# The zeros written ahead of the last 46 row gathers of a mixture-of-experts kernel are left out

## The reference

```python
h = _L0_tok_ref(x, w, b, gamma, beta, alpha)      # depthwise conv (5 taps, stride 2), group norm, PReLU
h = h + _L0_attn_ref(_layernorm(h), ...)          # state space scan over the positions, 16 states a channel
h = h + _L0_ffn_ref(_layernorm(h), ...)           # 64 experts, the two best for each token

# _L0_ffn_ref, for a token row xf:
logits = xf @ Wr + br
topk_logits, topk_idx = top_k(logits, 2)
gates = softmax(topk_logits)
y_e = relu(xf @ W1[e] + b1[e]) @ W2[e] + b2[e]    # for each chosen expert e
out = sum over the two chosen e of gate_e * y_e
```

## Time and profile before

| | before |
|---|---|
| median of three runs | 925.29 us |
| lowest and highest run | 922.06, 929.41 us |
| the profiled execution | 921.33 us |
| its span, first to last instruction | 919.6 us |
| busy in the span: POOL, DVE, PE, ACT | 71%, 62%, 60%, 36% |
| the 46 gathers of the third share, first start to last start | 840.64 to 909.36 us |
| last instruction of DVE ends | 912.56 us |

### The profile page before, as it was taken

How to read it: one execution, slowest core, us unless ns; L and a number is a source line. 1 busy time by engine, 2 the same in 40 slices (tenths; PEclk the granted TensorE clock), 3 DMA queues, 4 the chain that set the end, 5 groups by cost and what they waited for, 6 DMA issues and landing times.

```text
span 919.6 us, 9334 instructions
## 1 busy us (share of the span) xinstructions
PE 555.3 (60%) x2514; PEld 372.0 (40%) x2520; DVE 568.8 (62%) x1180; ACT 332.5 (36%) x622; POOL 654.9 (71%) x645
## 2 busy tenths in 40 slices
PE   4653347575674575768556756577679765794230
PEld 4642012122221221244324545565568554683230
DVE  1697899999999999876464511132234211247964
ACT  2169756466466554342132111122224211241010
POOL 5894699999999999706848888763740387503884
PEclk9967576898798887775767667798799875797565
DMA  7999900000000000002600344467578844651012
GB/s 238 384 156 116 44 0 0 0 0 0 0 0 0 1 0 0 0 1 75 162 14 26 112 137 131 129 171 206 151 207 227 240 133 119 173 151 43 22 56 70
DMA packets 106607, 84.98 MB, mean 92 GB/s; under 512 B 30464, under 2 KB 90240, under 8 KB 106560
## 3 DMA queue, kind: packets, MB, share of 16 engines
q1 hardware_dynamic: 79312, 54.76, 27.4%
q10 hardware_dynamic: 19184, 21.40, 7.4%
q0 software_dynamic: 8064, 8.27, 3.4%
HBM read 57.22 MB, written 33.49 MB: 99 GB/s over the span
## 4 chain that ended last, share of the span: by engine, by line
PE 32%; POOL 30%; issue 16%; DVE 10%; another core or an unknown queue 4%; ACT 4%; SPq 1%; DMA 1%; POOLq 0%; ACTq 0%; DVEq 0%
PE ps L894 15%; POOL x_w L570 12%; POOL w_ring L563 11%; PE ps L881 6%; POOL xt L634 5%; PE ps L870 2%; PE ps L659 2%; PE ps L723 1%; PE ps L750 1%; POOL beat L633 1%; PE ps L808 1%; PE ps L745 1%; DVE lstat L1280 1%; DVE mi L1498 1%
## 5 line engine op out<-in xcount | busy, mean ns | idle before, releaser
L723 PE MATMUL ps<-x_w,ident 128*128 128x512 f32 x252 | 154.3, 771 | 102.0 <-POOL x_w L570 102.0
L563 POOL TENSOR_TENSOR w_ring<-xt,bc 128x2016 f32<-128x2016 f32 x32 | 144.7, 4524 | 13.4 <-DVE hh_ring L1409 7.3
L634 POOL DMA_INDIRECT xt<-expert_out,slot_i x126 | 123.6, 981 | 37.0 <-issue 21.9
L613 POOL DMA_INDIRECT sorted_rows<-xp,slot_i x126 | 123.0, 976 | 35.9 <-issue 18.4
L1409 DVE TENSOR_TENSOR_SCAN hh_ring<-ps,w_ring 128x1024 f32<-128x1024 f32 x64 | 145.7, 2277 | 0.1
L570 POOL TENSOR_TENSOR x_w<-hh_ring,bc 128x2016 f32<-128x2016 f32 (+1 forms) x32 | 142.4, 4456 | 2.3 <-PE ps L723 2.3
L723 PEld LDWEIGHTS ps<-x_w,ident 128*128 128x128 f32 x252 | 60.0, 249 | 199.0 <-POOL x_w L570 125.7
L633 POOL MEMSET beat<- 128x128 f32 x126 | 27.5, 218 | 106.3 <-DMA expert_out<-x_w 106.1
L1603 DVE COPY x_w<-ps 128x256 f32<-128x256 f32 x80 | 33.9, 424 | 109.2 <-PE ps L894 58.8
L1060 ACT ACTIVATE ps<-dt_t,a_exp 128x1024 f32<-128x1024 f32 x64 | 71.5, 1117 | 63.7 <-DVE hh_ring L1409 63.6
L1054 ACT ACTIVATE ps<-dt_t,a_exp 128x1024 f32<-128x1024 f32 x64 | 71.5, 1118 | 51.9 <-DVE w_ring L1388 51.9
(11 more groups left out here) (211 smaller groups left out, 956.1 us busy)
## 6 DMA issues: line engine op xcount, KB each, us to landing
dt_t<-packed SPq DMA_DIRECT2D x140, 96.5 KB
x_w<-packed SPq DMA_DIRECT2D x112, 96.5 KB
x_w<-sorted_rows ACTq DMA_DIRECT2D x40, 256.0 KB
expert_out<-x_w ACTq DMA_DIRECT2D x80, 128.0 KB
sorted_rows<-pad_rows SPq DMA_DIRECT2D x2, 3584.0 KB, 24.2
bc<-packed SPq DMA_DIRECT2D x68, 96.5 KB
packed<-in_L_ffn_W SPq DMA_DIRECT2D x3, 2048.0 KB, 39.4
x_w<-in_x SPq DMA_DIRECT2D x7, 448.0 KB, 9.8
```

Source lines behind the costliest of these rows:

```text
L563: pool.tensor_tensor(w_buf(k, 2), up3[:, bass.ds(c * DC, DC), 1:S].unsqueeze(1).broadcast_to([P, 2, DC, L]), vec_of(k, 2), ALU.mult).then_ ...
L613: pool.indirect_dma_start(out=sorted_rows[h], out_offset=bass.IndirectOffsetOnAxis(ap=slot_i[:, c, l:l + 1], axis=0), in_=xn[:, l, :], in_ ...
L634: pool.indirect_dma_start(out=y[:, l, :], out_offset=None, in_=expert_out[h], in_offset=bass.IndirectOffsetOnAxis(ap=slot_i[:, c, l:l + 1] ...
L723: ins = pe.matmul(ps[:, i, :], ident[:, :], src[:, i * BANK:(i + 1) * BANK], start=(k < 0), stop=(k == (N - 2 if last else N - 1)), skip_g ...
```

## The change

The memset of `beat`, with its semaphore and wait, is left out ahead of the 46 gathers of the third share. The 46 gathers themselves, their order and their semaphores stay. The memsets ahead of the 126 sends and of the 80 gathers of the first two shares stay.

```diff
                         for l in range(a, z):
-                            ch.link(pool.memset(beat[:, :], 0.0))
+                            if h + 1 < len(SHARES):
+                                ch.link(pool.memset(beat[:, :], 0.0))
                             pool.indirect_dma_start(
                                 out=y[:, l, :], out_offset=None, in_=expert_out[h],
                                 in_offset=bass.IndirectOffsetOnAxis(ap=slot_i[:, c, l:l + 1], axis=0)
```

## The result

| | before | after |
|---|---|---|
| median of four runs | 925.9 us | 950.24 us |
| lowest and highest run | 922.06, 929.41 us | 948.70, 951.99 us |
| the profiled execution, its span | 921.33, 919.6 us | 950.14, 948.4 us |

The ratio is 1.0264, with a 95% interval of 1.0219 to 1.0309. The change makes the kernel 24.3 us slower; I had forecast 5 us less.

What follows compares the result with a forecast made beforehand. It took the end as a race that POOL's gathers lose to DVE by 5.07 us, DVE's chain then being the bound: 921.33 − 5.07 = 916.26 us, against the median 925.29 − 5.07 = 920.2 us; range 916 to 952.

Steps and rivals of the forecast that it cites:

- POOL: Third share's gathers: 46 memsets (10.1 us) and the gaps behind them (13.3 us) go, 23.4 us of POOL's time.
- the short end I chose: POOL, gather period: of bounds 0.957 and 2.62 us, the side of 0.957, the shortest gather record.
- the second possibility: POOL, gather period: 0.957 + 0.27 = 1.23 us if the release gap stays; DVE is then the bound.
- The rival of slower bare gathers: POOL, between gathers: directly following gathers are slower, over 1% from a period of 1.73 us, 49 us at 2.62; chance 0.40.
- p: POOL, third share: period from one gather's start to the next, 1.527 us before; up to 1.41 the full 5.07 is saved.
- Today's period: POOL: a gather needs 1.45 us whatever stands ahead; 921.8 us, up to 934.5; chance 0.10 for periods 1.41 to 1.73.
- DVE's waits for gathers: DVE, last group of three positions: two waits, 1.30 + 3.77 = 5.07 us, are saved.
- DVE's own: its present sequence without the two waits: DVE's end: 912.56 − 5.07 = 907.49, its chain otherwise unchanged.
- DVE is held up by gathers without gaps: DVE, line 1627: eight instructions each blocked for one 0.96 us gather, chain 7.7 us longer, 927.9 us; chance 0.03.
- What follows DVE's end stays: 7.04 us: Kernel's end: last store and end of program still take 919.6 − 912.56 = 7.04 us after DVE.

Runs made afterwards that it cites:

- few_incs: Changed kernel, but only the last of each gate table's 63 small DVE instructions raises its semaphore; 902.98 against 880.98 us for the kernel before, ratio 1.0255.
- early_tables_bare: Kernel before with gate tables built during the experts, two instructions a step, and no memsets ahead of the last 46 gathers; 895.42 us, ratio 1.0141.
- pace_256: Kernel before, but the last 46 gathers don't wait for their memset, which is longer (128 x 256); 885.63 against 883.43 us, ratio 1.0022.
- sp_raises: Kernel before, memsets kept, with SyncE raising a semaphore 700 times beside the last 46 gathers; 885.88 against 882.68 us, ratio 1.0052.
- sp_copies: Kernel before, memsets kept, with 32 plain copies of 32 KB on SyncE's queue beside the last gathers; 926.71 against 926.47 us, ratio 1.0022.
- late_wait: Kernel before, but the last 46 gathers don't wait for the memset ahead of them, the next memset does; 897.88 us, ratio 1.0193.
- bare_first12: Kernel before with the memset left out ahead of only the first 12 of the last 46 gathers; 882.53 us, ratio 0.999.
- wait_only: Kernel before, but ahead of the last 46 gathers POOL raises a semaphore and waits for it, with no memset; 904.56 us, ratio 1.0269.
- big_tables: Changed kernel, but each gate table is built by two large DVE instructions instead of 63 small ones; 905.81 us, ratio 1.0289 against the kernel before.

## Why the prediction was wrong, step by step

**POOL, right.** The memsets' 23.4 us are gone from POOL; 13.7 us of gaps between the gathers, 0.30 us each, have come in their place. The period of 1.256 us lies at the short end I chose, with the gap that I named as the second possibility (0.957 + 0.27 = 1.23). The Trainium skill, page Perfetto Trace Analysis, section "DMA Instruction — SWDGE (GPSIMD)", has the DSP complete the instruction after the record's end; the 0.30 us ahead of every gather, with nothing left there to wait for, fit that, but don't show it: a memset started behind a gather's record with no gap. The rival of slower bare gathers (0.40) had the sign of the result and a time near it, but p stayed far under its 1.73: it would have been right for a wrong reason. That the 950.24 us lie inside the stated 916 to 952 is luck, since the upper part of that range was this rival's. "Today's period" (p from 1.41) fell with it.

**DVE's waits for gathers, right.** They are gone, worth 5.14 us.

**"DVE's own: its present sequence without the two waits", wrong.** This is the step that failed. It took DVE's chain as given, and so as independent of how closely the gathers follow one another. In fact it grew by 31.67 + 5.92 us. The rival "DVE is held up by gathers without gaps" named the engine, but put it at line 1627 (now 1628), by a port lock, for 7.7 us, with a chance of 0.03. Its sign, a later start of that line, came, but from the tables ahead of it: line 1628 took its 4.90 us as before. D, contention for SBUF, doesn't explain the bare runs either. The delay starts 18 us after the first gather, not with it, ACT is late too in few_incs, and in early_tables_bare DVE stands still for 21 us with no instruction of its own running beside the gathers. So the lock that the Trainium skill describes (page SBUF — State Buffer, section "SBUF: two separate sides") is not what held DVE here.

**"What follows DVE's end stays: 7.04 us", wrong too, on the other side.** It fell to 2.04. This term was not DVE's but POOL's. The kernel closes with an instruction DRAIN on each engine. These are POOL's, before and then after (duration in ns, three times, then first and last start):

```profile
L136 POOLq DRAIN  x1: 10248/10248/10248, 909.1 to 909.1; - x1
L136 POOLq DRAIN  x1: 24097/24097/24097, 888.1 to 888.1; - x1
```

In both kernels POOL's DRAIN ends 10.0 us after the last gather's start. Before, that is at 919.4, 6.8 us behind DVE's end and 0.2 us ahead of the end of the span: the end was POOL's. After, it is at 912.2, long before DVE's end. In pace_256, where the last gather is late again, 880.0 − 873.03 = 6.97 us follow DVE's end. So even without the stall the sum would have missed: with p = 1.256 and DVE's chain as the prediction took it, the span would end at the later of 840.64 + 56.5 + 10.24 = 907.4 for POOL and 907.49 + 2.04 = 909.5 for DVE. That is an estimate from these rows, and 10 us less than the 919.6 before, not 5.07.

**What the trace of before had shown.** Its rounds of the bias additions grew from 0.64 us at 874 to 1.59 at 878, beside gathers; the last, at 883.95, was back at 0.81. This is DVE's timeline of the kernel before, between the lines of the earlier trace rows:

```profile
874.10 0.69 DVE L1643 TENSOR_TENSOR hg<-ps,hg 128x512 f32<-128x512 f32 x1 [0.64 <-PE ps L919]
...
877.93 0.69 DVE L1643 TENSOR_TENSOR hg<-ps,hg 128x512 f32<-128x512 f32 x1 [1.59 <-PE ps L919]
```

I read only that this stage ended in time. After the change, once the gathers had ended, the rounds are 0.64 us:

```profile
916.62 0.69 DVE L1644 TENSOR_TENSOR hg<-ps,hg 128x512 f32<-128x512 f32 x1 [0.64 <-PE ps L920]
```

In this case, hand-offs that lengthened beside a stream of transfers were the sign that the stream had little room left to come faster.

**What is shown, and what stays open.** Shown: the delay goes by the spacing of the indirect transfers (1.22 us: a ratio of 1.035; 1.26: 1.027; 1.36: 1.019; 1.50: 1.002), not by the wait or by the rows; it shows on DVE's small instructions 17 to 22 us after the first bare gather and on the hand-offs of DVE, PE and ACT from about 10 us on (early_tables_bare), grows while they run, and is gone some 4 to 8 us after the last (in after the last raise DVE waits for comes 909.10 − 902.22 = 6.9 us behind the last gather's start). It behaves like a backlog. Raises of others and small plain copies add a little to it. Not shown is what it queues in, or that it is a queue at all. Completion raises alone are too weak, by sp_raises and sp_copies, so something special to POOL's indirect transfers has the larger part. No run has gathers without completion raises. All these executions were recorded ones, and the recording may take part: of the 46 gathers' 736 completion raises the trace holds 610 in the kernel before and 640 in pace_256, but 229 in late_wait and 118 in the changed kernel. So most records of raises go missing where the engines stall. But sp_raises (243 left), bare_first12 (298) and sp_copies (381) miss about half or more of theirs with little or no loss of time, so the missing records don't follow the loss alone. Whether an unrecorded execution would stall as well can't be told from these runs. The Trainium skill, page NOTIFIC — the notification-queue block, section "7.1 Overflow: three behaviours, one of which stalls the engine", says that this block's internal pipeline always holds back its producers rather than lose a record; no run here shows whether that happened.

No version beat the kernel before. With all memsets POOL sets the end, by its last gather and the closing DRAIN; with too few DVE does. The best, bare_first12, can't be told from before.

## What to carry to other kernels

A spacer ahead of indirect DMAs that nothing reads may pace them for everyone else: before taking it out, look in the old trace whether other engines' hand-offs already lengthen beside the stream, as 0.64 to 1.59 us here. When a race between two engines decides a saving, price the change on the chain of the one that isn't changed too, for as long as it runs beside the faster stream, and look which engine the program's closing instructions wait for. Here 1.5 us from one indirect transfer to the next was enough, 1.36 us was not (1.9%), and 1.256 us cost 2.6%.

## What the hardware showed that I had not expected

- A semaphore that POOL raises and waits for itself adds nothing to the period: 1.26 us with it (wait_only), 1.256 without. The memset's 0.22 us and its release are what paced the gathers.
- Half the rows make a gather only 4% shorter: 0.913 against 0.951 us.
- Beside large DVE instructions with two inputs gathers stretch to the instruction's length. POOL's timeline in big_tables, where DVE's ran 4.3 us each; beside the short ones of the earlier trace rows it was up to 1.32 us:

```profile
813.64 4.10 POOL L635 DMA_INDIRECT xt<-expert_out,slot_i  x1 [0.30 <-issue]
818.04 3.97 POOL L635 DMA_INDIRECT xt<-expert_out,slot_i  x1 [0.30 <-issue]
```

- DVE can stand still between two small instructions that wait for nothing the profile shows: 32 gaps of up to 1.1 us, 28.0 us in all.
- POOL's closing DRAIN ends 10.0 us after the start of the last gather, some 7.7 us after that gather has landed in the kernel before (2.35 us).
